# Adding the two key halves of the exponentials on GpSimd ahead of the ones product of a fused attention block

## The reference

```
x = x + tanh(g_xattn) * mha(layernorm(x), ctx, ctx)
x = x + tanh(g_ffn)   * ffn(layernorm(x))
mha: q, k, v = projections with bias; softmax(q k^T / sqrt(32)) v, then Wo and bo
ffn: xq = fakequant(x); h = fakequant(silu(xq Wg^T) * (xq Wu^T)); h Wd^T   (weights rounded to 8 bits)
```

## Time and profile before

| what | value |
|---|---|
| median of three runs | 1784.08 us |
| profiled execution | 1786.49 us, of which the span from first to last instruction 1784.6 us |
| granted TensorE clock, mean | 0.963 |
| busy share PE / DVE / ACT / POOL | 91% / 73% / 47% / 31% |
| largest lines on PE in attention | L1217 to L1219 (projections), L1316 (`pv`), L1298 (scores) |
| L1316, value half / ones half | 2048 instructions each, busy 140.3 / 137.7 us |

### The profile page before, as it was taken

One profiled execution on the slowest core, in us unless ns is written; L12 is line 12 of the kernel. 1 busy time (PEld: TensorE's weight loads), 2 busy tenths in 40 slices (PEclk: granted clock), 3 DMA queues, 4 the chain that ended last, 5 costly groups with the idle time before them and its releaser, 6 DMA issues.

```text
span 1784.6 us, 33864 instructions
## 1 busy us (share of the span) xinstructions
PE 1622.6 (91%) x11880; PEld 766.5 (43%) x11880; DVE 1296.8 (73%) x2055; ACT 847.0 (47%) x1132; POOL 549.1 (31%) x782
## 2 busy tenths in 40 slices
PE   3849999999999999999999999955899999989888
PEld 2324444444444444444444444422444444434333
DVE  6716777776876777777768767657677878778666
ACT  3224435336335344354353362336677777757440
POOL 6114234235144243242351341212000000006778
PEclk7969999999999999999999999978899999999999
DMA  6658577586596586675775864453055543017996
GB/s 192 166 133 177 143 178 163 148 187 161 141 200 147 157 190 159 172 166 164 180 166 150 181 164 105 112 178 136 32 218 197 196 176 136 24 48 287 421 409 235
DMA packets 275019, 307.58 MB, mean 172 GB/s; under 512 B 152160, under 2 KB 201312, under 8 KB 272352
## 3 DMA queue, kind: packets, MB, share of 16 engines
q1 hardware_dynamic: 274912, 306.00, 61.3%
HBM read 176.17 MB, written 95.94 MB: 152 GB/s over the span
## 4 chain that ended last, share of the span: by engine, by line
PE 54%; issue 25%; DMA 7%; DVE 7%; POOL 3%; SPq 2%; ACT 2%; POOLq 0%; ACTq 0%; DVEq 0%
PE bank L1316 12%; PE bank L1217 12%; PE bank L1219 11%; PE bank L1218 11%; PE spair L1298 5%; DMA x<-out_dram 4%; POOL yh L628 3%; PE spair L1273 2%; DMA stacks<-mT 1%; ACT pr L671 1%; DVE ndev L961 1%; PE bank L1208 1%; DMA hb<-in_L_ffn_w_gate_dram 1%; DVE bst L869 1%; SPq L359 1%
## 5 line engine op out<-in xcount | busy, mean ns | idle before, releaser
L918 DVE TENSOR_REDUCE mx<-spair 128x4 f32<-128x1024 f32 x256 | 301.4, 1219 | 57.5 <-PE spair L1273 56.9
L671 ACT ACTIVATE pr<-spair 128x1024 f32<-128x1024 f32 x256 | 259.5, 1021 | 138.7 <-PE spair L1298 138.7
L896 DVE SCALAR_TENSOR_TENSOR parts<-bank,bqk,parts 128x512 f16<-128x512 f32 x128 | 96.0, 750 | 203.6 <-ACT parts L660 197.9
L1414 PE MATMUL spair<-xqT,wgT 128*128 128x512 bf16 x704 | 182.4, 382 | 1.2 <-ACT xqT L784 1.2
L1414 PE MATMUL spair<-xqT,wuT 128*128 128x512 bf16 x704 | 181.7, 381 | 0.0
L1298 PE MATMUL spair<-stacks 128*128 128x256 f16 x1024 | 154.1, 277 | 18.2 <-ACT pr L671 11.6
L660 ACT ACTIVATE parts<-bank,bqk 128x512 f16<-128x512 f32 x128 | 88.0, 688 | 172.9 <-PE bank L1219 172.9
L1316 PE MATMUL bank<-pr,v 128*32 128x256 f32 x2048 | 140.3, 392 | 29.0 <-DVE o L912 24.1
L767 ACT ACTIVATE sil<-spair,gsc 128x512 f32<-128x512 f32 x176 | 118.2, 680 | 75.2 <-PE spair L1414 75.2
L553 POOL TENSOR_TENSOR nw<-rt 128x4 f32<-128x4 f32 x96 | 21.1, 220 | 419.6 <-DVE rt L864 414.6
L628 POOL TENSOR_TENSOR yh<-yh,x 128x512 f32<-128x512 f32 x64 | 134.7, 2135 | 49.1 <-DMA x<-out_dram 29.9
(11 more groups left out here) (175 smaller groups left out, 3337.9 us busy)
## 6 DMA issues: line engine op xcount, KB each, us to landing
stacks<-qk_spill SPq DMA_DIRECT2D x384, 128.0 KB, 4.3
qk_spill<-parts SPq DMA_DIRECT2D x64, 512.0 KB, 3.1
x<-out_dram SPq DMA_DIRECT2D x32, 1024.0 KB, 10.9
h_spill<-hb SPq DMA_DIRECT2D x10, 2816.0 KB, 9.2
xbuf<-in_x_dram SPq DMA_DIRECT2D x16, 1024.0 KB, 7.1
cbuf<-in_ctx_dram SPq DMA_DIRECT2D x16, 1024.0 KB, 6.4
xres<-in_x_dram SPq DMA_DIRECT2D x16, 1024.0 KB, 5.6
out_dram<-xres SPq DMA_DIRECT2D x16, 1024.0 KB, 4.3
```

Source lines behind the costliest of these rows:

```text
L671: act.activation(pr[:, u % 4, :, :, :].rearrange("p a b q -> p (a b q)"), spair[u % 2][:, :, :].rearrange("p a q -> p (a q)"), ACT.Exp, sc ...
L896: dve.scalar_tensor_tensor(out=parts[:, c, 2 * w + 1, :], in0=pj[(g + 1) % 3][:, :], scalar=bqk[:, w, c:c + 1], in1=parts[:, c, 2 * w, :], ...
L918: dve.tensor_reduce(mx[:, h:h + 2, b, :], spair[u % 2][:, :, :].rearrange("p a (q k) -> p a q k", q=KH), AX_X, ALU.max).then_inc(max_done, 1)
L1414: last = pe.matmul(spair[k % 2][:, s, :], w[:, kc, t * P:t * P + P], xqT[:, par, kc, :], start=(kc == 0), stop=(kc == KC - 1))
```

## The change

The tile `ph` holds the sum of the two key halves of the exponentials. GpSimd makes it, one addition of 128x512 f32 for each half step (`add_halves`), 16 in a body. TensorE's `pv` does its 8 matmuls with the values as before, then waits for both additions of the step, and multiplies `ph` by the constants in 4 matmuls in place of 8. On GpSimd the two additions come first in each step, the low half of the output lags two steps in place of one, the low halves of x come one step later, and the four residual additions and the four low halves of a context come behind the last step. The high halves of the context on ScalarE move there too, and both now belong to the group after next (`far`), so the context is loaded near the start of SyncE's body. Before the loop the halves of context 2 are made.

```
...
+        ph = alloc(p1, "ph", [P, 4, 2, S], F32)
...
+                if more > 1:
+                    load_c(i + 2)
                 spill(i, 0)
...
+            def add_halves(j, u):
+
+                wait(pool, exp_done, j * NU + u + 1)
+                wait(pool, pv_mm, j * NGR + u // 2 + 1)
+                pool.tensor_tensor(ph[:, u % 4, :, :], pr[:, u % 4, :, 0, :], pr[:, u % 4, :, 1, :],
+                                   ALU.add).then_inc(halves_added, 1)
...
-            def body(j, nxt):
+            def body(j, nxt, far):
                 for g in range(NGR):
-                    if nxt is not None:
-                        if g < NT:
-                            low_c(nxt, g)
-                        else:
-                            low_x(nxt, g - NT)
-                    if g > 0:
-                        o_low(j, g - 1)
+                    add_halves(j, 2 * g)
+                    add_halves(j, 2 * g + 1)
+                    if g > 1:
+                        o_low(j, g - 2)
                     if g == 2 and nxt is not None:
                         x_rstds(nxt)
-                    if g >= NT:
-                        residual(j, g - NT)
+                    if g > NT and nxt is not None:
+                        low_x(nxt, g - NT - 1)
+                o_low(j, NGR - 2)
+                if nxt is not None:
+                    low_x(nxt, NT - 1)
                 o_low(j, NGR - 1)
+                for t in range(NT):
+                    residual(j, t)
+                if far is not None:
+                    for t in range(NT):
+                        low_c(far, t)
                 x1_rstds(j)
 
-            with pool.Fori(1, NG - 1) as i:
-                body(i - 1, i + 1)
-            body(NG - 2, None)
-            body(NG - 1, None)
+            for t in range(NT):
+                low_c(2, t)
+            with pool.Fori(1, NG - 2) as i:
+                body(i - 1, i + 1, i + 2)
+            body(NG - 3, NG - 1, None)
+            body(NG - 2, None, None)
+            body(NG - 1, None, None)
...
-            def body(i, j, nxt):
+            def body(i, j, nxt, far):
...
-                            high_c(nxt, g)
-                        else:
+                        if g >= NT:
...
                     for t in range(1, NT):
                         v_copy(i, t)
-
-            with act.Fori(1, NG - 1) as i:
-                body(i, i - 1, i + 1)
-            body(NG - 1, NG - 2, None)
-            body(None, NG - 1, None)
+                if far is not None:
+                    for t in range(NT):
+                        high_c(far, t)
+
+            for t in range(NT):
+                high_c(2, t)
+            with act.Fori(1, NG - 2) as i:
+                body(i, i - 1, i + 1, i + 2)
+            body(NG - 2, NG - 3, NG - 1, None)
+            body(NG - 1, NG - 2, None, None)
+            body(None, NG - 1, None, None)
...
-                for ones in (False, True):
-                    for kh in range(KH):
-                        for a in range(HPC):
-                            h = HPC * c + a
-                            at = S if ones else 0
-                            last = pe.matmul(obank[DK * a:DK * a + DK, at:at + S],
-                                             onesP[:, :] if ones else v[:, 2 * b + kh, DK * h:DK * h + DK],
-                                             pr[:, (2 * g + a // 2) % 4, a % 2, kh, :],
-                                             start=(kh == 0), stop=(kh == KH - 1))
+                for kh in range(KH):
+                    for a in range(HPC):
+                        h = HPC * c + a
+                        pe.matmul(obank[DK * a:DK * a + DK, 0:S], v[:, 2 * b + kh, DK * h:DK * h + DK],
+                                  pr[:, (2 * g + a // 2) % 4, a % 2, kh, :], start=(kh == 0), stop=(kh == KH - 1))
+                wait(pe, halves_added, j * NU + 2 * g + 2)
+                for a in range(HPC):
+                    last = pe.matmul(obank[DK * a:DK * a + DK, S:2 * S], onesP[:, :],
+                                     ph[:, (2 * g + a // 2) % 4, a % 2, :], start=True, stop=True)
                 last.then_inc(pv_mm, 1)
...
```

More of the change, by code:

```diff
@@ L191, in gated_block_kernel @@
         exp_done = sem("exp_done")
+        halves_added = sem("halves_added")
         pv_mm = sem("pv_mm")
@@ L423, in body @@
                     turn_c(i + 1, 1 - par)
-                if more > 1:
-                    load_c(i + 2)
                 spill(i, 2)
```

## The result

The changed kernel takes 1882.93 us, median of four runs (1881.00 to 1884.51); the kernel before took 1784.44 in the same series (four runs). The ratio is 1.0544, with a 95% interval of 1.0527 to 1.0561: slower, and inside the range; the forecast was 1861. The profiled execution has a span of 1882.6 us where before had 1784.6, so the spans differ by the same 98 us as the medians.

A forecast was written before the change was run, and what follows sets the result against it. TensorE, busy 91% and nearly gapless, was taken as the bound, so every wait is paid in full. Groups 1 to 13 add 74 us at 3.3 + 2.4 each, total +77: 1861 us, range 1808 to 1895.

The forecast's parts named there:

- The saving: TensorE's ones half keeps 8 of 16 instructions: 0.445 us saved a step, 3.56 us a group.
- The additions: 16 on GpSimd a group at 1.27 us each, hidden in ordinary steps but not in steps 0 and 3.
- First wait: Step 0: TensorE waits 3.47 us for sums behind the previous group's second-norm Newton operations on GpSimd.
- Second wait: Step 3: 2.9 us for sums behind the next group's first-norm Newton operations, plus 0.5 for normalisation; together 3.4 us.
- The clock: TensorE's clock drops after each of the two waits: 1.6 us, chance three in four each, 2.4 us a group.
- Groups 0, 14 and 15: Groups lacking one wait or bound elsewhere: group 0 +1, group 14 +1.1, group 15 0 us.
- The prologue: Before the loop, ScalarE makes context 2's halves before copying group 0's row maxima: 0 to 2.6 us later, taken as +1.2.
- Halves and residuals in the tail: Context halves and residual additions moved to the preceding body's end fit GpSimd's idle time; costed at nothing.
- a matter of the last stage alone: Additions stretched by GpSimd and VectorE contention, seen hardly in this stage; rival GpSimd the bound, 1962 us, chance 0.04.

The follow-up runs named there:

- pe_kept_busy: Changed kernel, with TensorE repeating the value product three more times in steps 0 and 3 to fill the pauses; 1843.0 us, ratio 1.0314.
- x1_behind: Changed kernel, with the second norm's twelve-operation Newton chain moved behind additions 0 and 1 of the next body; 1829.3 us, ratio 1.0238.
- adds_unused: Changed kernel, with all additions and moves kept but TensorE making the sums from the exponentials as before, never waiting for additions; 1786.9 us, ratio 1.0006.
- both_behind: Changed kernel, with both norms' Newton chains moved whole behind additions (0 and 1, 6 and 7); 1784.9 us, ratio 0.9989.
- step0_full: Changed kernel, Newton chains split over steps, x halves made later, step 0 with the old 8-matmul ones product and no additions; 1751.9 us, ratio 0.9809.
- steps_spread: Changed kernel, with each Newton chain cut into three single steps behind the additions of steps 0 to 2 and 3 to 5; 1764.1 us, ratio 0.9865.

## Why the prediction was right, point by point

**The saving.** The ones half to the next scores was 613.99 - 613.01 = 0.98 us and is 615.64 - 615.09 = 0.55: 0.43 a step for a forecast of 0.445, or 3.44 us a group.

**The additions.** 1297 ns for a forecast of 1.27 us, and hidden in six of eight steps. In step 2 the value half started 0.16 us late, behind VectorE's normalisation.

**First wait.** The forecast was 3.47 us, and the view says 3.47. Against a ones half that follows its value half by 0.89, as in ordinary steps, the delay is 587.02 - 582.48 - 0.89 = 3.65: the view counts from the modelled end of the value half, 0.18 us later.

**Second wait.** The forecast was 2.9 for the sums, and 0.5 more for the normalisation. The view says 2.95, or 3.16 by starts; the normalisation's wait grew by only 0.07, from 0.36 to 0.43. Without the clock a group then costs -3.44 + 3.65 + 3.16 + 0.07 + 0.16 = 3.6 us for a forecast of 3.3.

**The clock: the term that was mis-sized.** The prediction had 1.6 us a fall at a chance of three in four, 2.4 us a group. The fall came every time, 26 of 26. Its price in the body shown is (5.14 - 3.03) + (4.72 - 3.03) = 3.8 for the two stretches behind the pauses, and 0.46 for a ones half at the lower clock (588.03 - 587.02 against 0.55): 4.3 us. In the next group, with the short first fall, the same places sum to 2.9:

```profile
664.50 1.08 PE L1339 MATMUL bank<-ph,onesP 128*32 128x256 f32 x8 [3.48 <-POOL ph L574]
665.52 1.04 PE L1319 MATMUL spair<-stacks 128*128 128x256 f16 x4
...
669.47 0.60 PE L1319 MATMUL spair<-stacks 128*128 128x256 f16 x4
...
684.69 1.08 PE L1339 MATMUL bank<-ph,onesP 128*32 128x256 f32 x8 [2.96 <-POOL ph L574]
685.70 1.04 PE L1319 MATMUL spair<-stacks 128*128 128x256 f16 x4
...
689.80 0.60 PE L1319 MATMUL spair<-stacks 128*128 128x256 f16 x4
```

The mean by these rows is 3.6 us, and pe_kept_busy gives 3.4. The two parts check against the whole: the turnings of groups 1 to 14, at 193.2 and 1190.9 us, have 997.6/13 = 76.74 between them, where it was 69.69, so a group cost 7.05 us. pe_kept_busy, with the waits and without the falls, stands 73.34 - 69.69 = 3.65 above the kernel before, which is what the waits come to by the sum above (3.6), and the remaining 3.40 are the clock. The forecast had 2.4: 13 x 1.0 = 13 us of what was missing. The size of one fall was nearly right, 1.7 us (3.4/2) for 1.6; most of the error is the chance of three in four, since the fall came every time. In x1_behind the pause of step 3 brought a fall in nine of 13 groups, so 26 of 26 isn't a rule either. What decides it is open.

The Trainium skill (TensorE: Matmul & The Clock Gate, "HAM oscillation — how this bites in real kernels") describes a matmul kernel in which TensorE waits between its bursts of products and starts every next burst at the lower clock. The changed kernel agrees: its pauses of 3.47 and 2.95 us were followed by a fall each time, and filling them brought the clock back. x1_behind agrees only in part, with nine falls behind 13 such pauses.

**Groups 0, 14 and 15.** Forecast +1, +1.1 and 0; the periods give +1.2 (75.39 for 74.18), +1.2 (70.05 for 68.82) and 0.

**The prologue.** Forecast +1.2; the first turning is 4.0 us late. 3.8 of them arise far ahead of the halves of context 2, in the first q projections; TensorE's instructions up to there are the same in both kernels (timelines, the kernel before and then the changed one):

```profile
46.14 0.38 PE L1217 MATMUL bank<-xT,wqT 128*128 128x512 f16 x1 [0.95 <-DVE woT L855]
```

```profile
47.40 0.63 PE L1239 MATMUL bank<-xT,wqT 128*128 128x512 f16 x1
```

They begin at 47.02, 0.9 us later, and 14 of them start 0.43 us apart, as in the body's stretches at clock 0.50, where the kernel before has 0.22 throughout: 0.9 + 14 x 0.21 = 3.8. (The clock's own column reads 1.00 from 47.0 to 52.7 us, so the two views disagree here.) adds_unused has no such slow products, the other eight kernels with the change have 6 to 13. The kernel before has only one trace, so whether this is chance stays open; it isn't the term that the prediction had. That term came true and cost nothing: the copy of the maxima starts 119.56 - 117.84 = 1.72 us behind the turning, 114.19 - 113.79 = 0.40 in the kernel before, so 1.3 us later, but the first exponential starts 5.95 us behind the turning where it was 6.20.

**Halves and residuals in the tail.** Forecast at nothing; adds_unused shows it.

The sum of the forecast then fails at the clock (13 us), in the waits (13 x 0.3 = 4) and in a prologue that was late for another reason (3): 20 us, where 21 were missing in the spans and 22 in the medians. The mechanism was right, and what was mis-sized lay on one side.

## What to carry over

In this kernel the work that went from a full engine to an idle one was paid for not by the idle engine's load but by what stood in front of it in that engine's order. Look there for chains of small dependent operations, which cost their latency however little they compute, and cut them or put them behind what the full engine asks for. Price a pause of TensorE's not by its length alone: look in the trace for pauses of like length and what the products behind them took, and count how many of them had a fall at all. And each wait that is removed brings TensorE earlier to the next one (GpSimd's chain, then VectorE's normalisation, then its reductions), so expect a part of each gain to come back as a new wait.

## What the runs showed of the hardware

Small copies are stretched beside GpSimd's additions. VectorE's copy of 128x4 took 161 to 170 ns in all 16 cases before. Beside an addition it takes as long as the addition does: the copy that starts at 584.52, 0.04 us behind the addition of 584.48, took 1.25 us. The copy's line in the changed kernel, with minimum, median and maximum:

```profile
L979 DVE COPY rstd<-r x16: 155/1250/1251, 200.9 to 1339.4; 128x4 f32 x13, 128x4 f32<-128x4 f32 x3
```

The scaling of the residual (`ndev`, 128x512) shows it too, the more of it falls beside additions: 547 ns on average before, 666 in the changed kernel, 885 in both_behind, and

```profile
L994 DVE TENSOR_SCALAR ndev<-xres,mv,r 128x512 f32<-128x512 f32 x64 | 66.0, 1072 | 0.0
```

in step0_full. The additions themselves hardly suffer (1271 for a residual addition before, 1297 now). The prediction held this for a matter of the last stage alone; the Trainium skill (GPSIMD Engine Reference, "Key points") says that GpSimd shares its SBUF interfaces with VectorE and contends with its two-port instructions and those with two inputs in SBUF. The rows agree that the two hinder each other, on VectorE's side, while the additions' own mean moved by only 26 ns; whether the copy and the scaling are two-port instructions no run shows. In both_behind the copy is short again (156 ns on average) and the small operation of two inputs ahead of it long (999). That the first to meet an addition pays was not tested by itself.

In the changed kernel the clock falls at the same two places of every body from 1 to 13, and the length of the first fall alternates from group to group; what sets the alternation stays open. Pauses of one length don't always do the same: 2.93 to 2.98 us were followed by a fall in 12 of 12 groups of the changed kernel and in eight of 12 of x1_behind (groups 1 to 12 of both). Pauses of 0.7 to 1.8 us, as in both_behind and steps_spread, left the mean clock at 0.962 and 0.968, where it had been 0.963 before.
